# The first tokens on one queue in full rows, the first two output tiles one after the other, two late weight splits

## The reference, cut to what matters

```python
w = cond_weight[ids]                     # one 1024 x 1024 matrix out of 8 for each of 8 sequences
xc = einsum('bsi,boi->bso', x, w)        # x is (8, 256, 1024), float32
logits = xc @ W_router.T                 # 8 experts, rank 16
combine = top2(softmax(logits)), renormed
h = einsum('nd,erd->ner', xc, A_stack) * combine[..., None]
lora = einsum('ner,eor->no', h, B_stack) * 2.0
out = x + xc @ W_base.T + b_base + lora
```

## Time and profile before

| | |
|---|---|
| time, median of 3 runs | 399.78 us (399.42 to 399.96) |
| the profiled execution | 400.54 us, its span 398.7 us |
| PE busy | 391.8 us, 98% of the span |
| VectorE (DVE) busy | 302.0 us, 76% |
| ScalarE (ACT) busy | 183.9 us, 46% |
| DMA, mean | 183 GB/s |
| granted clock of PE | 1.00 over the span |

### The profile page before, as it was taken

The page is one execution under the profiler, slowest core; times in us unless marked ns, Lnnn a source line. Parts: engine busy times, 40 slices in busy tenths (PEclk is TensorE's granted clock), DMA queues, the critical chain, the costliest instruction groups (busy, mean ns, idle before and its releaser), DMA issues.

```text
span 398.7 us, 5684 instructions
## 1 busy us (share of the span) xinstructions
PE 391.8 (98%) x2184; PEld 332.3 (83%) x2184; DVE 302.0 (76%) x430; ACT 183.9 (46%) x281; POOL 39.9 (10%) x67
## 2 busy tenths in 40 slices
PE   7999999999999999999999999999999999999996
PEld 6788878888888888888888888888888888888885
DVE  3897876788799999964548787668868999997311
ACT  4786743758632445221146666257656224441000
POOL 0101100101000040011162000000000003101110
PEclk9999999999999999999999999999999999999999
DMA  7988791777530056476569977257084003632222
GB/s 234 369 315 312 282 353 58 251 251 265 185 105 0 29 183 188 157 258 215 193 217 366 354 230 264 96 165 230 27 264 156 5 0 111 197 117 79 81 79 79
DMA packets 21227, 72.96 MB, mean 183 GB/s; under 512 B 2832, under 2 KB 2848, under 8 KB 21200
## 3 DMA queue, kind: packets, MB, share of 16 engines
q1 hardware_dynamic: 15984, 56.11, 40.5%
q0 software_dynamic: 4928, 15.97, 11.4%
q10 hardware_dynamic: 288, 0.52, 0.4%
HBM read 64.20 MB, written 8.39 MB: 182 GB/s over the span
## 4 chain that ended last, share of the span: by engine, by line
PE 85%; DMA 5%; DVE 5%; ACT 2%; SPq 1%; issue 0%
PE bank_x L779 22%; PE bank_x L783 11%; PE bank_y L764 9%; PE bank_y L765 9%; PE bank_y L766 9%; PE bank_x L764 8%; PE bank_x L765 8%; PE bank_x L766 8%; DMA raw<-w_cond 4%; DVE wc_hl L521 3%; PE bank_y L823 2%; ACT wc_hl L459 2%; DMA raw<-x 1%; SPq L350 1%; DVE xp L664 1%
## 5 line engine op out<-in xcount | busy, mean ns | idle before, releaser
L779 PE MATMUL bank_x<-x_hl,wc_hl 128*128 128x512 f32 x512 | 129.0, 393 | 2.1 <-ACT wc_hl L477 2.1
L521 DVE TENSOR_TENSOR wc_hl<-raw,wc_hl 128x1024 fp32r<-128x1024 f32 x90 | 108.8, 1220 | 22.9 <-ACT wc_hl L459 22.9
L459 ACT CAST wc_hl<-raw 128x1024 fp32r<-128x1024 f32 x90 | 94.2, 1053 | 64.8 <-PE bank_y L766 35.0
L779 PEld LDWEIGHTS bank_x<-x_hl,wc_hl 128*128 128x128 f32 x512 | 92.1, 189 | 19.2 <-ACT wc_hl L477 2.7
L783 PEld LDWEIGHTS bank_x<-x_hl,wc_hl 128*128 128x128 f32 x512 | 70.1, 190 | 5.2
L783 PE MATMUL bank_x<-x_hl,wc_hl 128*128 128x256 f32 x512 | 71.7, 282 | 0.0
L411 POOL DMA_DIRECT2D out<-out_sb x28 | 15.3, 546 | 251.7 <-DVE out_sb L572 230.0
L564 DVE SCALAR_TENSOR_TENSOR out_sb<-bank_x,bias_sb,out_sb 128x512 f32<-128x512 f32 x32 | 23.5, 746 | 20.8 <-PE bank_x L766 15.4
L493 ACT CAST xc_hl<-xp 128x256 fp32r<-128x256 f32 x64 | 26.0, 406 | 25.0 <-DVE xp L664 24.9
L765 PE MATMUL bank_x<-x_hl,wc_hl 128*128 128x512 f32 x96 | 37.4, 390 | 0.0
L764 PE MATMUL bank_x<-x_hl,wc_hl 128*128 128x512 f32 x96 | 37.4, 390 | 0.0
(11 more groups left out here) (86 smaller groups left out, 479.0 us busy)
## 6 DMA issues: line engine op xcount, KB each, us to landing
raw<-w_cond SPq DMA_DIRECT2D x62, 512.0 KB, 4.7
raw<-w_base SPq DMA_DIRECT2D x24, 512.0 KB, 5.4
out_sb<-x POOLq DMA_DIRECT2D x32, 256.0 KB, 5.4
raw<-x SPq DMA_DIRECT2D x15, 512.0 KB, 5.1
out<-out_sb POOLq DMA_DIRECT2D x28, 256.0 KB, 2.3
raw<-w_cond SPq DMA_DIRECT2D x4, 256.0 KB, 5.0
out<-out_sb SPq DMA_DIRECT2D x4, 256.0 KB, 2.0
raw<-x ACTq DMA_DIRECT2D x2, 256.0 KB, 2.8
```

What stands on the lines that cost most here:

```text
L459: nc.scalar.copy(split_dst(key, HI), split_src(key)).then_inc(hi_done, 1)
L521: nc.vector.tensor_tensor(split_dst(key, LO), split_src(key), split_dst(key, HI).bitcast(F32), ALU.subtract).then_inc(lo_done, 1)
L779: nc.tensor.matmul(ps[:], wc_hl[:, slot_of(s, t), HI, k], x_hl[:, s % 2, k].rearrange("p h n -> p (h n)"), start=(k == 0), stop=False)
```

## The change

Five things are done. X0 and X1 are both issued by ScalarE, each as one transfer with 4 KB rows. SP issues W0 and W1 in two halves each, W0 first. The pieces are split in the order X0, X1, W0, W1, and PE does tile 0 whole (0, 0..7), then tile 1 in two halves. The dummy matmuls are 26 instead of 24. For odd s the splits of t = 6 move behind the last work on t = 7 (`late_splits`); for even s nothing changes. The small buffers (`wr_sb`, `const_sb`, `bias_sb`) get addresses behind the large ones, and `warm` comes before them.

```diff
@@ -53,17 +53,16 @@
 
 
 STARTS = 4
-START = [("x", 0, 0), ("w", 0, 0), ("w", 0, 1), ("x", 0, 1), ("w", 0, 2), ("w", 0, 3)]
-X0, W0, W1, X1 = range(STARTS)
-ACT_MOVES = [(X0, 0, 2), (X0, 2, 4)]
-SP_MOVES = [(W0, 0, 4), (W1, 0, 4), (X1, 0, 4), (W0, 4, 8), (W1, 4, 8)]
-HI_PIECES = [(X0, 0, 2), (X0, 2, 4), (W0, 0, 2), (W0, 2, 4), (W1, 0, 4), (X1, 0, 2), (X1, 2, 4), (W0, 4, 8),
+START = [("x", 0, 0), ("x", 0, 1), ("w", 0, 0), ("w", 0, 1), ("w", 0, 2), ("w", 0, 3)]
+X0, X1, W0, W1 = range(STARTS)
+ACT_MOVES = [(X0, 0, 4), (X1, 0, 4)]
+SP_MOVES = [(W0, 0, 4), (W0, 4, 8), (W1, 0, 4), (W1, 4, 8)]
+HI_PIECES = [(X0, 0, 2), (X0, 2, 4), (X1, 0, 2), (X1, 2, 4), (W0, 0, 2), (W0, 2, 4), (W0, 4, 8), (W1, 0, 4),
              (W1, 4, 8)]
-LO_PIECES = [(X0, 0, 2), (X0, 2, 4), (W0, 0, 2), (W0, 2, 4), (W1, 0, 4), (X1, 0, 2), (X1, 2, 4), (W0, 4, 8),
-             (W1, 4, 8)]
-
-START_STEPS = [(0, 0, 4), (1, 0, 4), (0, 4, 8), (1, 4, 8)]
-WARM, WARM_N = 24, 2 * P
+LO_PIECES = [(X0, 0, 2), (X0, 2, 4), (X1, 0, 2), (X1, 2, 4), (W0, 0, 4), (W0, 4, 8), (W1, 0, 4), (W1, 4, 8)]
+
+START_STEPS = [(0, 0, 8), (1, 0, 4), (1, 4, 8)]
+WARM, WARM_N = 26, 2 * P
 
 RESIDENT = {(0, 5): [("a", 0, 0)], (2, 5): [("b", 0, 0)]}
 
@@ -91,6 +90,13 @@
     if s % GSEQS == GSEQS - 1 and t >= 4:
         items = items + [("T" if t < 6 else "S", s // GSEQS, (P1, t % 2))]
     return items
+
+
+def late_splits(s, t):
+
+    if t < KT - 2 or s % 2 and t < KT - 1:
+        return []
+    return step_splits(s, KT - 2) + step_splits(s, KT - 1) if s % 2 else step_splits(s, t)
 
 
 def slot_of(s, t):
@@ -215,14 +221,15 @@
         a_hl = sb("a_hl", [P, 2, KT, P], F32R)
         b_hl = sb("b_hl", [P, 2, KT + HT, P], F32R)
 
-        wr_sb = sb("wr_sb", [P, KT, NR])
-        bias_sb = sb("bias_sb", [P, KT])
-        const_sb = sb("const_sb", [P, C_ALL])
         out_sb = sb("out_sb", [P, OUTS, PTOK])
         xc_low = sb("xc_low", [P, 2, TOK])
         h_sb = sb("h_sb", [P, PTOK])
         h_hl = sb("h_hl", [P, 2, 2, PTOK], F32R)
         gate_er = sb("gate_er", [P, NQ, EXPERTS, RANK])
+        warm = sb("warm", [P, WARM_N], F32R)
+        wr_sb = sb("wr_sb", [P, KT, NR])
+        const_sb = sb("const_sb", [P, C_ALL])
+        bias_sb = sb("bias_sb", [P, KT])
         logit_sb = sb("logit_sb", [P, NQ, NR])
         logit = logit_sb[:, :, 0:EXPERTS]
         shifted = sb("shifted", [P, NQ, EXPERTS])
@@ -233,7 +240,6 @@
         above = gate_er[:, :, :, 0:EXPERTS]
         equal = gate_er[:, :, :, EXPERTS:2 * EXPERTS]
         stat = sb("stat", [P, 5, NQ])
-        warm = sb("warm", [P, WARM_N], F32R)
 
         ident = const_sb[:, C_ID:C_ID + P]
         before = const_sb[:, C_TRI:C_TRI + EXPERTS * EXPERTS].rearrange("p (e j) -> p e j", e=EXPERTS)
@@ -492,9 +498,8 @@
                         act.wait_ge(xc_summed, c)
                         nc.scalar.copy(xc_hl[:, t, HI, s % 2 * TOK:(s % 2 + 1) * TOK],
                                        xp[:, s // 2 % 2, t, s % 2 * TOK:(s % 2 + 1) * TOK]).then_inc(xc_hi, 1)
-                        if t >= KT - 2:
-                            for key in step_splits(s, t):
-                                hi(key)
+                        for key in late_splits(s, t):
+                            hi(key)
                         if s % GSEQS == 2 and t == 2:
                             h_high(2 * g)
                     if s % GSEQS == 1:
@@ -646,8 +651,8 @@
             for key in START[STARTS:]:
                 lo(key)
 
-            def split_step(s, t):
-                for key in step_splits(s, t):
+            def split(keys):
+                for key in keys:
                     if key[0] == "bd":
                         b_raw = raw[:, LANDED["b", 0, 0][0]]
                         n = HT * P
@@ -664,13 +669,12 @@
                         nc.vector.tensor_tensor(xc, bank_x[t % HT][:, 0:TOK], xc_low[:, t % 2], ALU.add) \
                             .then_inc(xc_summed, 1)
                         if t < KT - 2:
-                            split_step(s, t)
+                            split(step_splits(s, t))
                         dve.wait_ge(xc_hi, c)
                         nc.vector.tensor_tensor(xc_hl[:, t, LO, s % 2 * TOK:(s % 2 + 1) * TOK], xc,
                                                 xc_hl[:, t, HI, s % 2 * TOK:(s % 2 + 1) * TOK].bitcast(F32),
                                                 ALU.subtract).then_inc(xc_lo, 1)
-                        if t >= KT - 2:
-                            split_step(s, t)
+                        split(late_splits(s, t))
                         if s % GSEQS == 2 and t == 2:
                             gate_h(2 * g)
                         if s % GSEQS == 2 and t == 3:
```

## The result

The changed kernel takes 397.48 us (median of 6 runs, 397.33 to 398.57) against 399.66 for the kernel before on the same chip: ratio 0.9946, 95% interval 0.9935 to 0.9958, so 2.2 us less. The forecast was 1.2 us less (398.6); the measured time lies 0.2 us under the low end of the range.

The account below looks back on a forecast made before the run. TensorE (PE), busy 98% of the span, was taken to set the end. Start 0.6 plus late splits 0.6 plus small buffers 0 gave 1.2 us less, 398.6 us as median, range 397.7 to 400.3.

Parts of the forecast that it names:

- The start: First tokens' stage: the new transfers and piece order bring the third output tile forward by 0.6 us, bounds +1.5 and -2.5.
- D: Gain of the start: how much earlier than 13.91 the third output tile begins, 6.80 - L, forecast +0.6 us.
- X1's time L: When ScalarE can begin X1's first rounding: forecast 6.2, from below 5.3, from above under 9.28; PE starts 1.51 later.
- W0's second half: Inside tile 0: must be usable by about 8.1; if it slips to 8.9, the start's gain loses 0.8 us.
- w(0,2): Weights for t = 2: rounded at 12.90 for a start at 13.91, 1.0 us of slack, letting D up to about 1.3 through.
- The rule of the Trainium skill: At the start: transfers from two engines interleave on the same 16 DMA engines, so W0 slows X1 while PE waits.
- The late splits: First router: moving a 1.14 us VectorE split behind the last sum removes PE's stall, +0.60 us, bounds 0 and 0.60.
- Small buffers last: Buffer addresses: moves addresses only, no row tells a cost by address; 0 us, a tenth of the 2.0 us store either way.
- PE's clock: Rival at the start: idle PE falls to its 1.2 GHz level, costing 2.0 us, result 400.6; chance 0.04.
- VectorE's later start in the product stages: Up to 1.14 us later against 2.1 us of slack, cost 0; rival that it binds, 399.2 to 399.6, chance 0.04.
- X1 was early, not late: Rival at the start: X1 late because both queues share the engines, at worst 401.7 us; chance 0.12.
- The dummies: Before PE's start: two extra dummy matmuls cost 2 x 0.10 us, end near 5.8, before PE could start; cost nothing.

Follow-up runs that it names:

- `h_hl` gaps: Changed kernel with a gap of 32, 64, 128 or 256 bytes per partition ahead of h_hl: 398.75, 399.47, 398.96, 397.76 us, one execution each.
- p_start: Kernel before with the new start alone (transfers, piece order, tile order, 26 dummy matmuls): 399.21 us, ratio 0.9983.
- r_whole_w: Changed kernel with W0 and W1 as one transfer each in 4 KB rows: 397.69 us, ratio 0.9945.
- q_h256: Changed kernel with a gap of 256 bytes per partition ahead of h_hl: 397.76 us, one execution.
- q_pad_before: Kernel before with bias_sb at 64 instead of 32 bytes per partition, so buffers behind it start 32 bytes further on: 400.61 us, ratio 1.0012.
- r_halves_x: Changed kernel with X0 and X1 in two halves each, four transfers of 2 KB rows on ScalarE's queue: 398.75 us, ratio 0.9976.

## Why the prediction came out as it did

**The start** (forecast +0.6 us, bounds +1.5 and -2.5): it pays, but the size came out right by luck. Alone it measures 0.7 us. Two terms of D = 13.91 - L - 7.11 were off and cancelled. X1's time L was 5.3, the lower bound, and not 6.2: PE started at 6.83 and t = 2 at 12.83, where the forecast had 7.7 and 13.3. And 13.91 was a late execution. Over the executions t = 2 starts between 12.95 and 13.91 with the old start (5 traces; mean 13.49) and between 12.48 and 13.11 with the new (9 traces: the changed kernel, its parts and the `h_hl` gaps; mean 12.82): 0.67 us, as the medians say, so one pair of traces, 1.08 us apart, overstates it. The rest went into waits behind PE's start. It starts at 6.86 on average, and 5.60 later would be 12.46, not 12.82. W0's second half took 0.4 back in the changed kernel's trace, the stall that the step had named. In four others t = 2 waits for w(0,2), which the step held to have 1.0 us of slack; in `p_start` ScalarE rounds it from 11.84 to 12.89 and PE starts at 12.94:
```profile
11.84 1.05 ACT L458 CAST wc_hl<-raw 128x1024 fp32r<-128x1024 f32 x1 [0.68 <-DMA raw<-w_cond]
12.94 2.08 PE L778 MATMUL bank_x<-x_hl,wc_hl 128*128 128x512 f32 x8
```
X1 was early, which goes with SP's matrix number arriving 0.7 us later than in the trace of before, so that X had the engines almost alone (422 GB/s in the slice of 3 to 4 us). The rule of the Trainium skill (DMA: Bandwidth & Descriptors, Issuing engines are not separate DMA queues), that two queues interleave on the same engines, goes with the 5.63 us of `r_whole_w`, one execution; it did not decide the sign.

**The late splits** (forecast +0.60 us): wrong in size. The sum took a wait out of one profiled execution as a fixed cost. It is there only when a weight transfer comes late: 0.60 and 0.2 us in two of six traces with the old order, nothing in four. The profiled execution had such a transfer, and took 400.54 us where the median was 399.78. The chain before the stall could have warned: ScalarE waited 1.27 us for a weight transfer until 47.43. The measured worth alone is 0.2 to 0.3 us, with an interval that holds 0.

**Small buffers last** (forecast 0, plus or minus 0.2): wrong, and the main cause of the miss: a term put at nothing. The step said that no row tells a cost by address. One did: the three forms of `h_hl` above, 399, 397 and 393 ns, the same for every matmul of a line, beside 389 to 392 for all but one of the other 512-column forms of the product stages. I had looked at the groups by line, where a mean over all operands hides them, and at the store, where nothing depends on it. Measured: 1.5 us.

**The rivals.** PE's clock did not fall in the profiled execution: the granted clock is 1.00 in each microsecond from 6 to 9 us, after 0.8 us of idle. VectorE's later start in the product stages was hidden, as computed: PE has no wait there. X1 was early, not late. The dummies ended at 5.99 here and at 6.97 in `q_h256`, not at 5.8, but in all nine traces PE starts 0.45 to 0.46 us behind the first rounding of W0, so they held nothing up.

**The sum** that would have been right: start 0.7, late splits 0 to 0.3, address 1.4 to 1.5, together 2.1 to 2.5, measured 2.2. (The low end of the range is 399.78 - 2.0 = 397.8 by its own terms, where the prediction has 397.7; the measured time lies under both.)

## What to carry to other kernels

Group matmuls by operand and shape, and compare the mean of forms that should be equal; a form that is 1 to 3% slower in every one of its instructions points at its operand, here at its start address; one whose mean is raised by a few long ones does not. A wait seen in one execution is a candidate, not a term of a sum: where the profiled run is slower than the median, say by how much each of its waits could be that difference. When a buffer's size is not a multiple of 256 bytes per partition, put it behind the large matmul operands.

## What the runs showed of the hardware

- A float32r matmul of 512 columns takes 389 ns in the trace when its moving operand starts at a multiple of 256 bytes in the partition, and on average 4 to 7 ns more at 32, 64 or 128 bytes past it (table above; one of the three forms at 128 takes 387). Those behind it pay too: at 32 bytes the five matmuls behind a triple take 1.16 us instead of 1.13. In all 32 triples cost 1.23 to 2.23 us, 13 to 23 ns for each matmul that reads the shifted buffer. Why 64 costs more than 32 and 128 is not known. Other types and column counts were not tried.
- SP's first read of the matrix number is not constant. In the changed kernel, beside ScalarE's two large transfers:
```profile
L356 SPq TENSOR_LOAD <-ids x1: 1322/1322/1322, 1.6 to 1.6; - x1
```
  and in the kernel before:
```profile
L350 SPq TENSOR_LOAD <-ids x1: 651/651/651, 1.6 to 1.6; - x1
```
  All traces of the new start, `r_halves_x` too, have SP's first issue at 3.42 to 3.59, four of five with the old one at 2.71 to 2.79 (the fifth, `q_pad_before`, at 3.56). In eleven traces with two 512 KB token transfers this read takes 1.32 to 1.42 us, in four with the old start 0.60 to 0.69. In `q_pad_before` and `r_halves_x` it takes 0.46, and the load of the address before it 1.84 and 1.87 instead of 0.84. So the new start goes with weights issued 0.7 us later; that this is contention with the token transfers was not tested by itself.
